# A last stage with two buffers each for mixed values and gates in place of four, and a sixth x1 tile kept in SBUF

## The chip, the core and the metric

The kernel runs on one core of one Trainium2 chip. The metric is the device time of one launch in microseconds, the median of several runs. The engines go by their usual short names: PE (TensorE), DVE (VectorE), ACT (ScalarE), POOL (GpSimd), SP (SyncE). SP computes nothing here: it issues transfers, one after the other, in the order of its program. ACT issues transfers too, between its own instructions. MB below is a million bytes; a tile of 128 partitions by 4,096 float32 values has 2.10 MB, which the profile writes as 2048 KB.

## The reference

The input x is one 512 x 512 image of 64 channels in float32. Two layers are added to it in turn:

```python
x = x + _L0_conv_ref(_gn(x), ...)   # group norm, five projections, einsum, layer norm, output projection, gate
x = x + _L1_conv_ref(_gn(x), ...)   # group norm, 12 x 12 Fourier modes times a complex weight, inverse transform
```

Layer 0 in its core is

```python
left  = (xn @ left_w  + left_b)  * mask * sigmoid(xn @ lgate_w + lgate_b)
right = (xn @ right_w + right_b) * mask * sigmoid(xn @ rgate_w + rgate_b)
out = einsum('bkjd,bkid->bijd', left, right)
out = (_ln(out, onorm_w, onorm_b) @ out_w + out_b) * sigmoid(xn @ ogate_w + ogate_b)
```

Its result x + out is called x1 below. Layer 1 needs sums over the whole of x1 (its low Fourier modes, its squares) before it can add anything to it.

## The kernel before

Five stages run one after the other, each in a block of its own:

- `prepare` reads x for the group norm's statistics and folds weights.
- `project` forms left, right and the output gate, and writes them to HBM (`lr_d`, `gate_d`).
- `contract` does the einsum for one channel after the other (64 of them) and writes the "mixed" values to `mixed_d`.
- `finish_layer0`, the stage that the change is about, forms x1.
- `layer1` takes the spectrum, and then adds the inverse transform to each tile of x1 and stores it to the output.

**SBUF.** The last three stages share one area of 196 KB in each partition, laid out by hand (class `Shared`, line 739; the second argument counts kilobytes). In the last stage but one it holds `XT` = 5 tiles of x (`xt`, 16 KB each, from 0), `MB` = 4 tiles of mixed values (`mt`, 4 KB each, from 80), 4 of gates (`gt`, 4 KB each, from 96), and behind them, from 112, the Fourier rows and smaller things. `contract` uses the bytes from 0 to 96 for its operands, and leaves 96 to 112 free.

**`finish_layer0`.** The image is cut into 128 groups (`GROUPS`) of four image rows, and four groups (`TG`) make one x tile; there are 32 tiles (`TILES`). A group is worked in two halves, and time is counted in slots n, one for each half. Group c needs its mixed values (0.52 MB), its gates (0.52 MB) and a quarter of an x tile (0.52 MB). In slot n:

- DVE does `gate(n)` (L1252), then `scale(n + 2)` (L1244), and in odd slots `add_x` of the group before (L1261). `scale` multiplies mixed values by the norm's scale; `gate` multiplies the projected values by the gates; `add_x` adds the turned result to the x tile, which thereby becomes x1.
- PE does the output projection of half n + 1 (L1154), spreads the norm's scale for half n + 3 (L1149), turns a finished group (L1160) in even slots, and, ten slots behind, does one eighth of the Fourier transform of an x1 tile (L1168).
- ACT squares each finished group (L1199). With the last group of tile k, in slot 8k + 9, it issues the store of that x1 tile to `x1_d` (L1202), if k < `KEPT`: the last `XT` tiles are never stored, and `layer1` takes them from SBUF.
- POOL adds up the squares (L1233).
- SP issues the loads. In odd slots it waits until `scale(n)` is done and loads the mixed values of group n // 2 + `MB` (L771), then waits until `gate(n)` is done and loads the gates of the same group (L774): one load each for the buffer just used. In slots n with n % 8 = 4 it loads x tile n // 8 + 2 (L768), if that is `XT` or above. In slots n with n % 8 = 6, once in seven tiles, it loads Fourier rows (L1137, 672 KB onto 28 partitions).

```python
            def slot(n):
                c = n // 2 + MB
                if n % 2 == 1 and c < GROUPS:
                    sp.wait_ge(m_scaled, n + 1)
                    mid.load_mixed(sp, c)
                    sp.wait_ge(y_gated, n + 1)
                    mid.load_gate(sp, c)
```

On DVE the order is gate(n), scale(n + 2), so in time SP issues the gates of one group and, 0.6 us later, the mixed values of the next. One such pair leaves in each group's time.

**The first loads** are issued in `contract`: the gates of the first `MB` groups and x tiles 0 and 1 beside the last channel (L870 to L875), x tile 2 (L882), the first `MB` mixed tiles (L885), and the x tiles from 3 to `XT` - 1 behind the last small transfers of the scale (L890).

**`layer1`** works through the 32 tiles in the order `TILE`, first those that are still in SBUF. It has `XR` = 10 tile buffers: the `XT` of the stage before and five more. `FREE` = 8: the loads of tiles `XT` to 7 of its order are issued at once (L1376), two more when the columns are ready (L1378), and every later one when a buffer has been stored (L1381).

Of the kernel before, what the change touches and what calls it, by code (L numbers as in the profile page):

```python
# [39 lines left out]
GW = RG * H  # L40
# [1 line left out]
RING = 4  # L42
UB = 2 * BG
UNITS = L // 2
XT = 5
MB = 4
AREA = 196 * 256
DIRECT = 4
BATCH = 7
# [40 lines left out]
class Tools:  # L90


    def __init__(self, nc, ctx, phase):
        self.nc, self.ctx, self.phase = nc, ctx, phase
# [644 lines left out]
class Shared:  # L739

    def __init__(self, t, x, mixed_d, gate_d):
        self.nc = t.nc
        self.base = t.nc.sbuf_base
        t.sb("area", [P, AREA])
        self.xt = [self.at("fi", f"x{b}", 16 * b, [TG, WS, C]) for b in range(XT)]
        self.mt = [self.at("fi", f"m{b}", 80 + 4 * b, [GW]) for b in range(MB)]
        self.gt = [self.at("fi", f"g{b}", 96 + 4 * b, [GW]) for b in range(MB)]
        self.rows = self.at("fi", "rows", 112, [M2, TG * C])
        self.st = self.at("fi", "s", 136, [RG, GW], F32R)
        self.pick = self.at("fi", "pick", 174, [P // 4, P], F32R)  # L750
        self.basis_rows = self.at("fi", "basis_rows", 190, [WS, RG * M2])
        self.x_loaded = [t.sem(f"x_loaded{b}") for b in range(XT)]
        self.m_loaded = [t.sem(f"m_loaded{b}") for b in range(MB)]
        self.g_loaded = [t.sem(f"g_loaded{b}") for b in range(MB)]
        self.s_loaded = t.sem("s_loaded")
        self.basis_loaded = t.sem("basis_loaded")
        self.x_v = x.rearrange("a h w c -> (a h w c)").rearrange("(n g p f) -> n p g f", g=TG, p=P, f=WS * C)
        self.m_v = mixed_d.rearrange("e d (n r) j -> n (e d) (r j)", r=RG)
        self.g_v = gate_d.rearrange("e d (n r) j -> n (e d) (r j)", r=RG)
# [7 lines left out]
    def load_x(self, sp, k):  # L767
        sp.dma_start(self.xt[k % XT].rearrange("p g t c -> p g (t c)"), self.x_v[k]).then_inc(self.x_loaded[k % XT], DMA)  # L768

    def load_mixed(self, sp, c):  # L770
        sp.dma_start(self.mt[c % MB], self.m_v[c]).then_inc(self.m_loaded[c % MB], DMA)  # L771

    def load_gate(self, sp, c):
        sp.dma_start(self.gt[c % MB], self.g_v[c]).then_inc(self.g_loaded[c % MB], DMA)  # L774

# [4 lines left out]
def contract(nc, lr_d, mixed_d, basis_rows, keep, mid):  # L780
# [4 lines left out]
    with ExitStack() as ctx:  # L785
# [63 lines left out]
        def spread_part(eng, part, source, e):  # L849

            for q in range(RG):
                rows = slice(P // 4 * q, P // 4 * q + P // 4)
                at = P // 2 * part + P // 4 * e
                eng.dma_start(mid.st[at:at + P // 4, q, :].bitcast(F32),
                              source[rows, e, :, :].rearrange("p t j -> p (t j)").bitcast(F32)).then_inc(mid.s_loaded, DMA)

        @block.sync
        def _(sp):
# [28 lines left out]
            for e in range(2):  # L887
                sp.wait_ge(low_ready, e + 1)
                spread_part(sp, 1, s_low, e)
            for k in range(3, XT):  # L890
                mid.load_x(sp, k)
# [156 lines left out]
def finish_layer0(nc, x1_d, fourier_d, keep, mid):  # L1048
# [6 lines left out]
    TILES = GROUPS // TG  # L1055
    KEPT = TILES - XT
    with ExitStack() as ctx:
# [16 lines left out]

        x1_stored = [t.sem(f"x1_stored{b}") for b in range(XT)]
        f_stored = [t.sem(f"f_stored{b}") for b in range(2)]
# [206 lines left out]
def layer1(nc, x1_d, w_real, w_imag, inverse_rows, inverse_columns, out, keep, mid):  # L1283
# [7 lines left out]
    GR = L // NG  # L1291
    GP = P // NG
    NTG = GROUPS // TG
    XR = XT + 5
    SPLIT_O = 40
    FREE = XT + 3
    KEPT = NTG - XT
    TILE = [(KEPT + n) % NTG for n in range(NTG)]
    CB = L // GR
    with ExitStack() as ctx:  # L1300
# [17 lines left out]
        col = mid.at("la", "col", 112, [GR, C])  # L1318
        span = TG * WS * C
        xt = [mid.xt[(KEPT + b) % XT].rearrange("p g t c -> p (g t c)") for b in range(XT)]  # L1320
        xt += [mid.at("la", f"x{b}", at, [span]) for b, at in enumerate((80, 96, 176, 144, 160))]
        ps = [t.ps(f"ps{k}", [P, L]) for k in range(8)]
        f_ps = [ps[a][0:C, 0:NM * M2] for a in range(2)]
        s_ps = ps[2][0:C, :]
# [3 lines left out]
        inv_loaded = t.sem("inv_loaded")  # L1328
        loaded = [t.sem(f"loaded{b}") for b in range(XR)]
        stored = [t.sem(f"stored{b}") for b in range(XR)]  # L1330
        step = t.sem("step")
# [21 lines left out]
        def by_group(tile):  # L1353
            return tile.rearrange("p (g f) -> p g f", g=TG)
# [12 lines left out]
        def _(sp):  # L1367
# [5 lines left out]
            def load(n):  # L1373
                sp.dma_start(by_group(xt[n % XR]), x_v[TILE[n]]).then_inc(loaded[n % XR], DMA)

            for n in range(XT, FREE):  # L1376
                load(n)
            sp.wait_ge(col_ready, C // CB)  # L1378
            for n in range(FREE, XR):
                load(n)  # L1380
            for n in range(XR, NTG):  # L1381
                sp.wait_ge(stored[n % XR], DMA * (n // XR))
                load(n)
# [131 lines left out]
def program(nc, ins, tab, out):  # L1515
# [6 lines left out]
    with ExitStack() as ctx:  # L1522
# [28 lines left out]
        with ExitStack() as back:  # L1551
            m = Shared(Tools(nc, back, "back"), x, mixed_d, gate_d)
            contract(nc, lr_d, mixed_d, tab["t_basis_rows"], k, m)
            finish_layer0(nc, x1_d, fourier_d, k, m)
            layer1(nc, x1_d, ins["L1_conv_w_real"], ins["L1_conv_w_imag"], tab["t_inverse_rows"],
                   tab["t_inverse_columns"], out, k, m)
# [20 lines left out]
```

## Time and profile before

| | us |
|---|---|
| median of three runs | 2878.99 |
| lowest and highest run | 2877.46, 2883.83 |
| the profiled execution | 2879.03 |
| its span in the trace | 2877.2 |

| stage | stretch of the span, us |
|---|---|
| `prepare` and `project` | 0 to about 1050 |
| `contract` | to 1828 |
| `finish_layer0` | 1828 to 2498 |
| `layer1` | to 2877 |

The trace is one execution on the core; times in it are counted from the span's start. A transfer has two times: when its queue issues it, and how long after that it has landed; the profile gives the second as "us to landing". "DMA share" in a table of stretches is the mean busy share of the core's 16 DMA engines (it can be a little over 1), and GB/s is what they moved.

### The profile page before, as it was taken

The numbers are of one execution on the slowest core, as the hardware profiler recorded it, in microseconds if no ns is written. First come the engines' busy times: TensorE is split into PE (matmuls) and PEld (weight loads), VectorE is DVE, ScalarE is ACT, GpSimd is POOL, SyncE is SP. The second block draws the span as 40 slices with busy tenths as digits, with TensorE's granted clock in tenths as the row PEclk, the third lists the DMA queues.
The fourth block names the chain that finished last, engine by engine and source line by source line (L and its number), as shares of the span: only waits on it lengthen the run. The fifth ranks groups of instructions, "written<-read, shape, count | busy, mean of one in ns | idle before, by whom it ended". The sixth has DMA issues, their size and how long they took to land. (4 is left out here: it accounts for less than half of the span.)

```text
span 2877.2 us, 44035 instructions
## 1 busy us (share of the span) xinstructions
PE 2459.1 (85%) x14742; PEld 2000.9 (70%) x14742; DVE 2216.7 (77%) x3468; ACT 1380.9 (48%) x1812; POOL 1021.6 (36%) x1043
## 2 busy tenths in 40 slices
PE   0008999889989969999999999599998999979983
PEld 0007998778778858888888887366665666778872
DVE  6998999779779848888888888777676767427852
ACT  0107999779779966676766766122221222100000
POOL 0019988788788820000000000244443444300000
PEclk9999999999999989999999999799999999859996
DMA  9945999888888876777777777999999999539999
GB/s 384 391 166 194 351 349 348 305 329 310 318 310 329 315 274 249 277 280 288 275 287 273 284 281 270 347 391 416 393 415 391 415 384 399 146 126 386 420 421 408
DMA packets 244985, 927.61 MB, mean 322 GB/s; under 512 B 18010, under 2 KB 21594, under 8 KB 244443
## 3 DMA queue, kind: packets, MB, share of 16 engines
q1 hardware_dynamic: 205912, 796.12, 73.4%
q10 hardware_dynamic: 38898, 129.21, 11.3%
q8 instruction: 105, 1.72, 0.2%
q14 instruction: 70, 0.57, 0.1%
HBM read 527.85 MB, written 394.92 MB: 321 GB/s over the span
## 5 line engine op out<-in xcount | busy, mean ns | idle before, releaser
L1233 POOL TENSOR_TENSOR fi_square_sum<-fi_square_sum,fi_square 128x1024 f32<-128x1024 f32 x128 | 302.9, 2366 | 361.1 <-ACT fi_square L1199 361.1
L717 DVE SCALAR_TENSOR_TENSOR pj_lr<-pj_v_ps,keep_b_val,pj_sig 128x1024 f32<-128x1024 f32 x256 | 328.6, 1283 | 128.3 <-PE pj_v_ps L570 97.8
L912 PE MATMUL ct_acc_ps<-ct_l_hi,ct_r_hi 128*128 128x512 f32 x1024 | 404.4, 395 | 26.7 <-DVE ct_r_lo L989 26.7
L914 PE MATMUL ct_acc_ps<-ct_l_hi,ct_r_lo 128*128 128x512 f32 x1024 | 404.2, 395 | 0.0
L913 PE MATMUL ct_acc_ps<-ct_l_lo,ct_r_hi 128*128 128x512 f32 x1024 | 404.2, 395 | 0.0
L1199 ACT ACTIVATE fi_square<-fi_x 128x1024 f32<-128x1024 f32 x128 | 135.5, 1058 | 519.0 <-DVE fi_x L1261 516.5
L510 POOL TENSOR_TENSOR front_ring<-front_ring,front_gn_shift 128x512 f32<-128x512 f32 x256 | 330.4, 1292 | 31.8 <-DVE front_ring L683 31.8
L653 ACT ACTIVATE pj_sig<-pj_g_ps,keep_b_gate 128x1024 f32<-128x1024 f32 x256 | 285.9, 1117 | 42.3 <-PE pj_g_ps L570 37.6
L1154 PE MATMUL fi_y_ps<-fi_scaled,keep_w_bd 128*128 128x512 f32 x512 | 273.5, 616 | 30.0 <-DVE fi_scaled L1244 29.6
L1244 DVE TENSOR_TENSOR fi_scaled<-fi_m,fi_s_ps 128x512 f32<-128x512 f32 x256 | 174.2, 681 | 135.9 <-DMA fi_m<-mixed_d 125.8
L1225 POOL MEMSET fi_square_sum<- 128x1024 f32 x1 | 1.0, 952 | 758.8 <-POOLq L785 758.8
L530 POOL TENSOR_TENSOR front_ring<-front_ring,pj_guess 128x512 f32<-128x512 f32 x256 | 267.7, 1047 | 3.3 <-POOL pj_guess L524 1.6
L1168 PE MATMUL fi_f_ps<-fi_x,fi_basis_rows 128*96 128x256 f32 x1024 | 264.3, 382 | 0.0
L563 PE MATMUL pj_x_ps<-pj_high,front_minus 64*128 64x512 f32 x512 | 257.6, 503 | 0.2
L570 PE MATMUL pj_o_ps<-pj_high,front_w_og_high 64*128 64x512 f32 x512 | 249.4, 487 | 0.1
L912 PEld LDWEIGHTS ct_acc_ps<-ct_l_hi,ct_r_hi 128*128 128x128 f32 x1024 | 198.1, 193 | 68.5 <-issue 27.1
L1430 PE MATMUL la_ps_ps<-la_col,keep_mask_row 128*128 128x256 f32 x1024 | 229.2, 387 | 13.7 <-DVE la_x L1508 9.7
L1149 PE MATMUL fi_s_ps<-fi_s,fi_pick 128*128 128x512 f32 x256 | 208.1, 814 | 36.0 <-DMA fi_s<-ct_s_low 36.0
L692 DVE BATCH_NORM_STATS2 pj_stats<-front_ring 128x6 f32<-128x128 f32 x1024 | 227.6, 287 | 5.4 <-POOL front_ring L510 5.4
L554 PE MATMUL pj_x_ps<-keep_ident,front_ring 64*128 64x64 f32 x2048 | 209.8, 223 | 25.5 <-POOL front_ring L530 24.7
L1430 PEld LDWEIGHTS la_ps_ps<-la_col,keep_mask_row 128*128 128x128 f32 x1024 | 198.2, 194 | 44.5 <-DVE la_x L1508 11.5
L554 PEld LDWEIGHTS pj_x_ps<-keep_ident,front_ring 64*128 64x128 f32 x2048 | 204.3, 140 | 34.2 <-POOL front_ring L530 25.0
(183 smaller groups left out, 6315.1 us busy)
## 6 DMA issues: line engine op xcount, KB each, us to landing
lr_d<-pj_lr SPq DMA_DIRECT2D x128, 1024.0 KB, 6.6
gate_d<-pj_gout SPq DMA_DIRECT2D x128, 512.0 KB, 7.1
ct_l<-lr_d SPq DMA_DIRECT2D x64, 1024.0 KB, 7.0
ct_r<-lr_d SPq DMA_DIRECT2D x64, 1024.0 KB, 9.0
mixed_d<-ct_o SPq DMA_DIRECT2D x64, 1024.0 KB, 5.0
fi_g<-gate_d SPq DMA_DIRECT2D x128, 512.0 KB, 14.8
fi_x<-in_x SPq DMA_DIRECT2D x32, 2048.0 KB, 17.2
fi_m<-mixed_d SPq DMA_DIRECT2D x128, 512.0 KB, 17.5
```

Source lines behind the costliest of these rows:

```text
L510: pool.tensor_tensor(tile(m), tile(m), keep.gn_shift[:, :].unsqueeze(1).to_broadcast([P, WS // 2, C]), ALU.add).then_inc(shifted, 1)
L530: pool.tensor_tensor(tile(m), tile(m), root, ALU.mult).then_inc(xn_ready, 1)
L554: last = pe.matmul(x_ps[m % 2][:, columns], pair, keep.ident[side(e), side(e)], start=(e == 1 and i == 0), stop=False, is_transpose=True, ...
L653: act.activation(sig[m % 2][:, :], g_ps[:, :], ACT.Sigmoid, bias=keep.b_gate[:, 0:1]).then_inc(sig_ready, 1)
L717: dve.scalar_tensor_tensor(out=out[:, :, RG * (m % 2):RG * (m % 2) + RG], in0=v_ps[:, :].rearrange("p (q i) -> p q i", i=RG), scalar=keep. ...
L912: pe.matmul(bank, high, l_hi[b][:, :, k, :], start=(k == 0), stop=False)
L913: pe.matmul(bank, high, l_lo[b][:, :, k, :], start=False, stop=False)
L914: last = pe.matmul(bank, low, l_hi[b][:, :, k, :], start=False, stop=(k == WT - 1))
L1154: pe.matmul(y_ps[n % 2], keep.w2_bd[:, :], scaled[n % 2], start=True, stop=True).then_inc(y_ready, 1)
L1168: last = pe.matmul(f_ps[k % 2], mid.basis_rows[:, s, :], xt[k % XT][:, :, s, :], start=(s == 0), stop=(s == WS - 1))
L1233: pool.tensor_tensor(square_sum[:, :, :], square_sum[:, :, :], square[:, :, :], ALU.add).then_inc(sum_done, 1)
L1430: last = pe.matmul(bank[:, :, s % 2, :], inv_cols[:, s, :], col[:, TG * TILE[n]:TG * TILE[n] + TG, :], start=True, stop=True)
```

## The change

The number of x tiles goes from 5 to 6 and that of the mixed and of the gate tiles from 4 to 2 each. The sixth x tile takes the 16 KB from 80 to 96; the mixed tiles move to 96 and 100, the gate tiles to 104 and 108. `layer1` drops its own tile buffer at 80, and keeps ten in all; `FREE` stays 8. So SP issues a mixed and a gate load two groups ahead in place of four; 26 x1 tiles are stored in place of 27, and 26 are loaded again in `layer1` in place of 27.

```diff
@@ -42,8 +42,8 @@
-XT = 5
-MB = 4
+XT = 6
+MB = 2
 AREA = 196 * 256
@@ -743,8 +743,8 @@
         self.xt = [self.at("fi", f"x{b}", 16 * b, [TG, WS, C]) for b in range(XT)]
-        self.mt = [self.at("fi", f"m{b}", 80 + 4 * b, [GW]) for b in range(MB)]
-        self.gt = [self.at("fi", f"g{b}", 96 + 4 * b, [GW]) for b in range(MB)]
+        self.mt = [self.at("fi", f"m{b}", 96 + 4 * b, [GW]) for b in range(MB)]
+        self.gt = [self.at("fi", f"g{b}", 104 + 4 * b, [GW]) for b in range(MB)]
         self.rows = self.at("fi", "rows", 112, [M2, TG * C])
@@ -1291,9 +1291,9 @@
-    XR = XT + 5
+    XR = XT + 4
     SPLIT_O = 40
-    FREE = XT + 3
+    FREE = XT + 2
@@ -1318,7 +1318,7 @@
         xt = [mid.xt[(KEPT + b) % XT].rearrange("p g t c -> p (g t c)") for b in range(XT)]
-        xt += [mid.at("la", f"x{b}", at, [span]) for b, at in enumerate((80, 96, 176, 144, 160))]
+        xt += [mid.at("la", f"x{b}", at, [span]) for b, at in enumerate((96, 176, 144, 160))]
```

## Rows read from the trace of the kernel before

**Rows 1.** The page: the span, and each engine's busy time.

```profile
span 2877.2 us, 44035 instructions
PE 2459.1 (85%) x14742; PEld 2000.9 (70%) x14742; DVE 2216.7 (77%) x3468; ACT 1380.9 (48%) x1812; POOL 1021.6 (36%) x1043
```

**Rows 2.** Stretches: length, busy time by engine, granted clock, DMA share, GB/s.

```profile
1900.00:1940.00 40.00, 40.00 (x187) 27.98 (x185) 32.31 (x43) 9.23 (x10) 19.50 (x9) 1.00 1.02 414
...
2060.00:2100.00 40.00, 39.28 (x181) 26.77 (x180) 29.24 (x39) 9.20 (x10) 18.25 (x9) 1.00 1.03 417
...
2550.00:2600.00 50.00, 38.11 (x281) 36.69 (x282) 23.92 (x30) 7.12 (x12) 4.37 (x1) 0.70 0.16 57
```

**Rows 3.** Waits, 1830 to 2480: who for whom, us, times, longest.

```profile
DVE fi_scaled L1244 <- DMA fi_m<-mixed_d: 125.8, 59, 8.1
```

**Rows 4.** Timeline of DVE: start, duration; scale at groups 8 and 127.

```profile
1859.76 0.68 DVE L1244 TENSOR_TENSOR fi_scaled<-fi_m,fi_s_ps 128x512 f32<-128x512 f32 x1
...
2477.97 0.68 DVE L1244 TENSOR_TENSOR fi_scaled<-fi_m,fi_s_ps 128x512 f32<-128x512 f32 x1
```

**Rows 5.** Timeline of DVE: scale in three following groups, near 1894.

```profile
1890.37 0.68 DVE L1244 TENSOR_TENSOR fi_scaled<-fi_m,fi_s_ps 128x512 f32<-128x512 f32 x1
...
1893.26 0.68 DVE L1244 TENSOR_TENSOR fi_scaled<-fi_m,fi_s_ps 128x512 f32<-128x512 f32 x1
...
1898.05 0.68 DVE L1244 TENSOR_TENSOR fi_scaled<-fi_m,fi_s_ps 128x512 f32<-128x512 f32 x1
```

**Rows 6.** Timeline of SP's queue, the same place: when transfers are issued.

```profile
1885.69 0.33 SPq L774 DMA_DIRECT2D fi_g<-gate_d  x1
1886.29 0.33 SPq L771 DMA_DIRECT2D fi_m<-mixed_d  x1
...
1890.93 1.14 SPq L768 DMA_DIRECT2D fi_x<-in_x  x1
1892.12 1.43 SPq L771 DMA_DIRECT2D fi_m<-mixed_d  x1
```

**Rows 7.** DMA issues, single: mixed 1886.29, store 1887.43, mixed 1892.12 (KB, us to landing).

```profile
fi_m<-mixed_d SPq DMA_DIRECT2D x1, 512.0 KB, 4.6
...
x_d<-fi_x ACTq DMA_DIRECT2D x1, 2048.0 KB, 9.7
...
fi_m<-mixed_d SPq DMA_DIRECT2D x1, 512.0 KB, 12.0
```

**Rows 8.** Timeline of DVE: scale at the start of groups 114 to 116.

```profile
2417.90 0.69 DVE L1244 TENSOR_TENSOR fi_scaled<-fi_m,fi_s_ps 128x512 f32<-128x512 f32 x1 [3.07 <-DMA fi_m<-mixed_d]
...
2421.55 0.68 DVE L1244 TENSOR_TENSOR fi_scaled<-fi_m,fi_s_ps 128x512 f32<-128x512 f32 x1
...
2425.31 0.68 DVE L1244 TENSOR_TENSOR fi_scaled<-fi_m,fi_s_ps 128x512 f32<-128x512 f32 x1
```

**Rows 9.** Stretches, columns as in Rows 2: a PE gap, and what follows it.

```profile
2177.90:2182.10 4.20, 0.05 (x2) 0.01 (x1) 0.75 (x2) 0.00 (x0) 0.00 (x0) 0.83 1.01 237
...
2182.10:2187.50 5.40, 5.40 (x10) 2.97 (x10) 2.99 (x4) 1.06 (x1) 1.90 (x1) 0.50 0.98 328
2036.90:2040.40 3.50, 0.00 (x1) 0.00 (x0) 0.71 (x2) 0.00 (x0) 0.00 (x0) 1.00 1.02 419
2040.70:2044.10 3.40, 3.40 (x7) 1.80 (x7) 2.72 (x4) 1.06 (x1) 0.17 (x1) 0.50 1.03 418
```

**Rows 10.** Timeline of SP's queue: loads around a load of Fourier rows.

```profile
2013.50 0.79 SPq L774 DMA_DIRECT2D fi_g<-gate_d  x1
2014.39 1.30 SPq L1137 DMA_DIRECT2D fi_rows<-fourier_d  x1
2015.74 0.96 SPq L771 DMA_DIRECT2D fi_m<-mixed_d  x1
```

**Rows 11.** DMA issues, single: the gate load of 2013.50, the mixed load of 2015.74.

```profile
fi_g<-gate_d SPq DMA_DIRECT2D x1, 512.0 KB, 19.5
...
fi_m<-mixed_d SPq DMA_DIRECT2D x1, 512.0 KB, 23.9
```

**Rows 12.** Timeline at the stage's start: x tiles 3 and 4, the next mixed load, scale of group 2.

```profile
1826.36 1.20 SPq L768 DMA_DIRECT2D fi_x<-in_x  x2
...
1831.09 0.34 SPq L771 DMA_DIRECT2D fi_m<-mixed_d  x1
...
1837.21 0.68 DVE L1244 TENSOR_TENSOR fi_scaled<-fi_m,fi_s_ps 128x512 f32<-128x512 f32 x1
```

**Rows 13.** DMA issues, single: the mixed load of 1831.09.

```profile
fi_m<-mixed_d SPq DMA_DIRECT2D x1, 512.0 KB, 9.8
```

## The prediction

> **What bounds the kernel now.** I read the page first [rows 1]. PE is the busiest engine over the whole span, 2459.1 of 2877.2 us, but the change touches one stage and a half, so I went to stretches of that stage [rows 2]. From 1900 to 1940 PE is busy all the time (40.00 of 40.00): PE sets the pace. From 2060 to 2100 it isn't (39.28), DVE neither (29.24), and the DMA engines stand at a share of 1.03 and 417 GB/s: the bytes set the pace. The waits say the same from the other side: DVE's `scale` stood still for mixed values for 125.8 us in 59 waits [rows 3].
>
> The PE's own pace is 4.79 us for a group, read between two starts of `scale`, 1893.26 and 1898.05 [rows 5]. From group 8 to group 127 the stage took 2477.97 - 1859.76 = 618.2 us [rows 4]; 119 groups at 4.79 would be 570.0, so what is lost to DMA today is 48.2 us. The bytes of a tile of four groups are 4.2 MB of mixed values and gates, 2.1 of x and 2.1 of the store: 8.4 MB, 20.1 us at 417 GB/s against 19.2 on PE. Today's stage is thus within a few per cent of both limits, and it gets there because four buffers let requests pile up.
>
> **The change: the wait that it adds.** With two buffers, the mixed load for group c can only leave when `scale` of group c - 2 is done. In the stretch that PE paces, one `scale` ends at 1890.37 + 0.68 = 1891.05, and the `scale` that would need that load starts at 1898.05 [rows 5]: 7.0 us are left for it. With four buffers two more groups, 9.6 us, come on top. How long does such a load take? Alone behind its gate load it lands after 4.6 us, in time. But the mixed load of 1892.12 was issued right behind an x load, with the store of an x1 tile (landing after 9.7) on ACT's queue, and took 12.0 [rows 6, 7]. The queues were nearly empty before it, since the load of 1886.29 needed 4.6. That is the very state in which two buffers would always find them. It landed at 1904.12, that is 6.1 us after 1898.05. Behind the waiting `scale` stand all later DVE instructions of the group; PE waits for their `scaled` and `gated`, and SP's next pair of loads waits for them too. So the waiting shuts off requests: the DMA engines, which have no gap in mid stage today, are idle for a few microseconds in every tile.
>
> **Price of a tile with both an x load and a store.** I take the loop that closes on itself. From the gate load that precedes the store, 1885.69, to the landing at 1904.12 are 18.4 us [rows 6, 7]. The bytes on this way are 0.52 x 4 for two pairs, 2.1 of x and 2.1 of the store: 6.3 MB, 15.1 us at 417 GB/s, so at the very best 15.1 and 2.7 us of fixed time (the load that landed at 1890.89 is 5.2 after 1885.69, with 2.5 us of bytes): 17.8. Then from the late `scale` to the next such gate load: the other half's `scale` and one group more. By DVE's rate after a wait, 3.65 for a group (2417.90 to 2421.55 [rows 8]), that is some 5.0 us; by PE's pace, 4.79, up to 6.8. The loop is 22.8 at best, 24.7 where I take the observed 18.4 and 6.3. I take more than 5.0 because of PE's clock: a PE gap of 4.2 us was followed by 5.4 us at a granted clock of 0.50 and one of 3.5 by 3.4 us at 0.50 [rows 9], which is the lower of its two levels (1.2 in place of 2.4 GHz) and costs half of that stretch, 1.7 to 2.7. The upper end is 18.4 + 6.8 + 1.7, some 27.0. Against 19.2 for four groups of PE, such a tile loses 5.5 us (3.6 to 7.8).
>
> **How many.** x tiles 6 to 31 are now loaded in the stage, at tiles 4 to 29; tiles 0 to 25 are stored, each one tile later. Both fall together at tiles 4 to 26: 23 times 5.5 = 127 us (83 to 179).
>
> **Tiles 27 to 29, an x load and no store.** Gates, x and mixed values are 7.6 us of bytes, and 2.7 fixed, 10.3 after the gate load's issue, where 7.6 are available: 2.7 late. After a wait two groups ran at 3.65 and 3.76 in place of 4.79 [rows 8], which wins back 2.2. I take 1 each, 3 in all (0 to 6). Tiles 1 to 3, with a store alone, I cost at nothing: 1 MB of loads beside the store is covered by the 7.0 us and the 2.2 that can be won back; without that cover it would be some 2 each.
>
> **Fourier rows.** The gate load of 2013.50 landed after 19.5, the mixed load of 2015.74 after 23.9 [rows 10, 11]: 6.6 us apart, with the rows between them, and 1.3 of it the mixed load's own. So the rows hold SP's queue for 5.3 us. Three of the four times this comes one pair behind an x load, where nothing is left to win back: 3 x 5.3 = 16, and 3 for the last one: 19 (12 to 30).
>
> **The start.** x tiles 3 and 4 are issued at 1826.36, the next mixed load at 1831.09 lands 9.8 later, at 1840.9 [rows 12, 13]. Now it is group 2's, which `scale` wants at 1837.21, and x tile 5 (2.1 MB, 5.0 us) is in front of it: 1845.9, so 8.7 us late; 9 (8 to 12). Two gate loads fewer in `contract` move nothing, since PE there waits for the scale.
>
> **What the change saves.** One store of 2.1 MB is 5.0 us of bytes; in a stage whose DMA engines now have gaps that is worth nothing, in today's it would be 5.0. In `layer1` one load is gone, but of those issued before the columns are ready; from 2550 to 2600 the share is 0.16 [rows 2], so it hid in an idle stretch. From there on the stage loads 24 tiles and stores 32, as before. I take 0 (a gain of 5 at most).
>
> **Sum.** 127 + 3 + 19 + 9 = 158 us lost, less the 48.2 lost today: +110, on the profiled execution's 2879.03 (span 2877.2, about 1.8 around it): 2989. That execution is within 0.1 us of the median of the runs, 2878.99. With all low ends: 83 + 0 + 12 + 8 - 48 - 5 = +50, 2929. With all high ends: 179 + 6 + 30 + 12 - 48 = +179, 3058.
>
> **What the notes say.** The Trainium skill ("Trainium Kernel Development and Optimization", Best Practices) advises to double-buffer so that DMA overlaps with compute. By that, two buffers hide the loads and only the saved bytes count; this is the third rival below. The trace speaks against it: 12.0 us of latency stand against 7.0 of lead [rows 5, 7]. The same skill ("Perfetto Trace Analysis", Optimization Strategy) reads a gap that repeats on the engine that should be saturated as a possible lack of buffers; it fits the added wait, not today's, which come at a DMA share of 1.03 [rows 2].
>
> **The rivals.**
> - *The clock holds.* The waits come as I say, but PE's gaps stay short enough, and DVE goes on at its own rate behind each wait: the loop is 18.4 + 5.0 = 23.4, 4.2 a tile, 23 x 4.2 = 97. Sum 97 + 3 + 19 + 9 - 48 = +80, 2959. For it: waits of 3.07 us did not slow the groups behind them [rows 8]. Against it: a PE gap of 3.5 did [rows 9], and my wait is 6.1, of which PE has work left for about two. Chance 0.28.
> - *The clock falls in full each time*, and the loop is 27: 23 x 7.8 = 179, 179 + 3 + 19 + 9 - 48 = +162, 3041. For it: the 4.2 gap cost 2.7. Chance 0.15.
> - *The bytes are the bound anyway, and there are fewer of them.* The requests are fewer at a time but never too few; the stage keeps its pace, and the store that is gone is worth its 5.0: 2874, faster than before. It decides in the loop above: with 5.0 from the late `scale` to the next pair, the way from pair to landing would have to be 20.1 - 5.0 = 15.1, the bare bytes with no fixed time at all. The single trace of it says 18.4. Chance 0.05.
> - *The change doesn't do what it says:* the load that goes was idle time's, the one that comes at the start is not. That part is in my sum (9 us); alone, with no waits, it would give some +4, 2883. Chance 0.03.
>
> **How the numbers follow.** My forecast, 2989, has 0.49. It and the two cases on its sides hold 0.92. The range goes from 2920, below the low ends, to 3060, the high ends; what it leaves out is the last two rivals and a tail above, together some 0.12. This kernel can be told from no change at about 0.2%, 6 us. Faster by more: 0.03, most of the third rival. Within: 0.03. Slower: 0.94.
>
> **What would show it.** In the trace of the changed kernel: waits of DVE's `scale` for mixed loads near 6 us, once in a tile, 250 us or more in total in place of 125.8; a period of `scale` near 24.7 us for four groups in mid stage; a DMA share below 1 and near 350 GB/s there; a median latency of the mixed loads under 10 us in place of 17.5, though each wait is longer; PE's clock at 0.50 for some microseconds in each tile; a first wait of about 9 us in group 2; `layer1` as long as before. I am wrong if the share stays at 1.03 in mid stage, or if the mixed load behind x lands in less than 8 us: then the lead of 7.0 was enough.

## The result

The changed kernel takes 3013.15 us, median of four runs (3007.66 to 3020.91), beside 2878.22 for the kernel before (four runs, 2872.17 to 2883.83): a ratio of 1.0474, 95% interval 1.0457 to 1.0491. That is 135 us slower. The forecast was 110 slower, 2989, in a range of 2920 to 3060. Its profiled execution is the fastest of the four, 3007.66 (span 3005.8), so 128.6 us of span are to be explained.

Nearly all of it lies in `finish_layer0`, whose first `scale` starts 0.8 us earlier than before. From `scale` of group 127 to the end of the span it is 399.2 us in the changed kernel and 399.3 before. From group 8 to group 127 it is 2606.57 - 1871.16 = 735.4 us in place of 618.2 [rows 4]: 117.2 more. The first eight groups take 12.2 more.

The page of the changed kernel, in the lines that answer to [rows 1], with the loads' medians (KB, us to landing):

```profile
span 3005.8 us, 44032 instructions
PE 2500.7 (83%) x14742; PEld 2023.6 (67%) x14742; DVE 2219.6 (74%) x3468; ACT 1379.5 (46%) x1812; POOL 1020.7 (34%) x1043
...
fi_g<-gate_d SPq DMA_DIRECT2D x128, 512.0 KB, 4.7
fi_x<-in_x SPq DMA_DIRECT2D x32, 2048.0 KB, 12.5
fi_m<-mixed_d SPq DMA_DIRECT2D x128, 512.0 KB, 7.0
```

A single mixed load is much quicker than before, 7.0 us in place of 17.5, and the kernel is slower. A latency says nothing until it is held against the lead with which the load was asked for. Stretches of the stage, columns as in [rows 2]:

```profile
2060.00:2100.00 40.00, 29.53 (x110) 19.14 (x111) 21.00 (x29) 5.55 (x6) 11.81 (x5) 0.83 0.87 302
...
2060.00:2400.00 340.00, 280.89 (x1137) 186.72 (x1138) 197.47 (x260) 59.71 (x65) 122.38 (x52) 0.89 0.88 327
```

The longer of them in the kernel before:

```profile
2060.00:2400.00 340.00, 317.90 (x1403) 212.97 (x1402) 237.71 (x318) 72.45 (x79) 150.26 (x64) 0.98 1.02 404
```

No engine is busy all the time now, and neither are the DMA engines: a share of 0.88 and 327 GB/s, where the kernel before has 1.02 and 404 over the same 340 us. The granted clock is 0.89 over the stretch, 0.98 before. The waits of the stage (us in total, times, longest), with [rows 3] for the first; the second and third are PE waiting for DVE's late `scale`:

```profile
DVE fi_scaled L1244 <- DMA fi_m<-mixed_d: 166.8, 36, 9.7
PEld fi_y_ps L1154 <- DVE fi_scaled L1244: 130.3, 36, 9.1
PE fi_y_ps L1154 <- DVE fi_scaled L1244: 115.6, 31, 9.0
DVE fi_gated L1252 <- PE fi_y_ps L1154: 70.8, 81, 2.4
...
DVE fi_gated L1252 <- DMA fi_g<-gate_d: 39.8, 26, 3.3
```

Fewer waits (36 in place of 59), but long ones, and a second kind that the forecast did not have: gates that come late, 26 times.

One turn of the loop, as SP and ACT issue it (start, duration):

```profile
2017.73 0.33 SPq L774 DMA_DIRECT2D fi_g<-gate_d  x1
2018.33 0.33 SPq L771 DMA_DIRECT2D fi_m<-mixed_d  x1
...
2019.47 0.37 ACTq L1202 DMA_DIRECT2D x_d<-fi_x  x1
...
2022.54 0.33 SPq L774 DMA_DIRECT2D fi_g<-gate_d  x1
2022.98 1.11 SPq L768 DMA_DIRECT2D fi_x<-in_x  x1
2024.13 1.44 SPq L771 DMA_DIRECT2D fi_m<-mixed_d  x1
...
2027.93 0.33 SPq L771 DMA_DIRECT2D fi_m<-mixed_d  x1
2038.17 0.33 SPq L774 DMA_DIRECT2D fi_g<-gate_d  x1
...
2044.27 0.33 SPq L774 DMA_DIRECT2D fi_g<-gate_d  x1
```

The same six transfers from 2017.73 to 2024.13, each asked for by itself (KB, us from issue to landing), in that order:

```profile
fi_g<-gate_d SPq DMA_DIRECT2D x1, 512.0 KB, 3.6
fi_m<-mixed_d SPq DMA_DIRECT2D x1, 512.0 KB, 4.8
...
x_d<-fi_x ACTq DMA_DIRECT2D x1, 2048.0 KB, 10.1
fi_g<-gate_d SPq DMA_DIRECT2D x1, 512.0 KB, 8.0
fi_x<-in_x SPq DMA_DIRECT2D x1, 2048.0 KB, 12.5
fi_m<-mixed_d SPq DMA_DIRECT2D x1, 512.0 KB, 12.6
```

And DVE, which waits for the last of them, and before that for the gates (in brackets its idle time and what ended it):

```profile
2030.56 0.75 DVE L1252 SCALAR_TENSOR_TENSOR fi_gated<-fi_y_ps,keep_c_col,fi_g 128x512 f32<-128x512 f32 x1 [1.53 <-DMA fi_g<-gate_d]
2036.79 0.69 DVE L1244 TENSOR_TENSOR fi_scaled<-fi_m,fi_s_ps 128x512 f32<-128x512 f32 x1 [5.48 <-DMA fi_m<-mixed_d]
...
2043.48 0.75 DVE L1252 SCALAR_TENSOR_TENSOR fi_gated<-fi_y_ps,keep_c_col,fi_g 128x512 f32<-128x512 f32 x1 [2.36 <-PE fi_y_ps L1154]
```

From the gate load at 2017.73 to the landing at 2036.7 are 19.0 us, from there to the next such gate load, 2044.27, 7.5: a loop of 26.5. Over 22 such loops in the trace the means are 19.1 and 7.1, 26.2 in all. Between 2027.93 and 2038.17 SP issues nothing: it stands behind DVE.

What PE's clock does meanwhile (stretches; the columns as above):

```profile
2033.30:2037.40 4.10, 0.01 (x1) 0.00 (x0) 0.61 (x2) 0.00 (x0) 0.00 (x0) 0.89 1.03 417
2037.50:2043.30 5.80, 5.77 (x10) 3.04 (x11) 3.62 (x5) 1.06 (x1) 2.27 (x1) 0.50 0.62 218
```

PE stood still for 4.1 us and then worked 5.8 us at a granted clock of 0.50 (1.2 GHz), while the DMA share sank to 0.62 because nothing had been asked for. The trace holds 23 such stretches between groups 8 and 127, 133 us in sum; the kernel before has 4, 20.5 us. In this turn `gate` then waits for PE (the 2.36 above): that is where the clock gets onto the path.

### The profile page after: what moved, and what is told of

The parts are those of the page before. It is cut to its first block and busy times, and to the rows that moved or that the text cites. A ratio compares the mean times of both kernels' runs of the same rounds, so it can differ in the third digit from the quotient of the medians.

```text
span 3005.8 us, 44032 instructions
## 1 busy us (share of the span) xinstructions
PE 2500.7 (83%) x14742; PEld 2023.6 (67%) x14742; DVE 2219.6 (74%) x3468; ACT 1379.5 (46%) x1812; POOL 1020.7 (34%) x1043
## 3 DMA queue, kind: packets, MB, share of 16 engines
q1 hardware_dynamic: 205384, 794.02, 70.8%
## 5 line engine op out<-in xcount | busy, mean ns | idle before, releaser
L1154 PE MATMUL fi_y_ps<-fi_scaled,keep_w_bd 128*128 128x512 f32 x512 | 300.3, 672 | 115.7 <-DVE fi_scaled L1244 115.6
L1244 DVE TENSOR_TENSOR fi_scaled<-fi_m,fi_s_ps 128x512 f32<-128x512 f32 x256 | 173.9, 680 | 175.7 <-DMA fi_m<-mixed_d 166.8
L1252 DVE SCALAR_TENSOR_TENSOR fi_gated<-fi_y_ps,keep_c_col,fi_g 128x512 f32<-128x512 f32 x256 | 191.7, 749 | 134.0 <-PE fi_y_ps L1154 70.8
L1168 PE MATMUL fi_f_ps<-fi_x,fi_basis_rows 128*96 128x256 f32 x1024 | 279.2, 399 | 0.0
L1149 PE MATMUL fi_s_ps<-fi_s,fi_pick 128*128 128x512 f32 x256 | 224.2, 876 | 36.0 <-DMA fi_s<-ct_s_low 36.0
L554 PE MATMUL pj_x_ps<-keep_ident,front_ring 64*128 64x64 f32 x2048 | 209.7, 223 | 25.4 <-POOL front_ring L530 24.7
```

What stands on the lines that cost most here:

```text
L1154: pe.matmul(y_ps[n % 2], keep.w2_bd[:, :], scaled[n % 2], start=True, stop=True).then_inc(y_ready, 1)
L1168: last = pe.matmul(f_ps[k % 2], mid.basis_rows[:, s, :], xt[k % XT][:, :, s, :], start=(s == 0), stop=(s == WS - 1))
```

## The experiments

All times are medians. Gains and losses are told as distances to the kernel before on the same chip: the changed kernel is 135 us above it. The ratio is to the kernel before on the same chip. Its median was 2873.3 beside the first four experiments (both kernels with five tiles, x loads in quarters in front, x loads on ACT's queue), 2874.0 beside the next four (small x loads, small stores, sixth tile later, all spread), and 2875.5 beside the last four. "Period" is the time from one `scale` to the one four groups later, as a mean over the 21 tiles from group 20 to group 103, those with Fourier rows included: 21.3 us in the kernel before, 26.2 in the changed one. The small x loads and the small stores leave something out of the result; all other kernels compute all of it. "Start" is the time from the first `scale` to that of group 8: 30.0 before, 42.2 changed.

| kernel | us | ratio (95%) | period | start |
|---|---|---|---|---|
| the change | 3013.2 | 1.0474 (1.0457 to 1.0491) | 26.2 | 42.2 |
| two buffers, five tiles | 3019.2 | 1.0497 (1.0473 to 1.0520) | 26.6 | 38.3 |
| three buffers, five tiles | 2886.7 | 1.0046 (1.0029 to 1.0063) | 21.8 | 29.6 |
| x loads in quarters, in front | 2962.2 | 1.0308 (1.0290 to 1.0325) | 24.7 | 42.6 |
| x loads on ACT's queue | 2917.6 | 1.0156 (1.0139 to 1.0173) | 22.3 | 42.8 |
| small x loads | 2856.7 | 0.9941 (0.9926 to 0.9956) | 19.9 | 42.7 |
| small stores | 2884.6 | 1.0038 (1.0024 to 1.0051) | 21.0 | 39.0 |
| sixth tile later | 3003.8 | 1.0475 (1.0454 to 1.0495) | 26.2 | 40.7 |
| all spread | 2887.7 | 1.0051 (1.0037 to 1.0064) | 21.5 | 38.5 |
| stores in quarters | 3016.3 | 1.0487 (1.0470 to 1.0504) | 26.6 | 43.8 |
| x loads in quarters, behind | 2908.7 | 1.0112 (1.0096 to 1.0127) | 22.3 | 41.6 |
| all spread, ahead | 2881.1 | 1.0022 (1.0012 to 1.0031) | 21.1 | 37.8 |
| the same, four buffers, five tiles | 2874.3 | 0.9997 (0.9988 to 1.0007) | 21.1 | 28.8 |

### Which part of the change

Two buffers alone, and three:

```diff
-MB = 4
+MB = 2        # XT stays 5
```

> The kernel before with two buffers each for mixed values and gates, and still five x tiles: the change without its sixth tile. Theory (a lead of about 7 us for a mixed load that takes 12 to 14 behind an x load, beside a store): the whole loss is there, less the late start of the changed kernel (11 us), plus two more tiles with both an x load and a store at some 6.5 us each: 3010 to 3020. Rival A (the sixth tile's load, ahead of the first mixed loads, and its new places are what costs): it falls back to 2880 to 2900.

Measured 3019.2, as expected: the loss is all there without the sixth tile. Rival A falls; neither the sixth tile nor the new places of the buffers are what costs, and the tiles run at 26.6 us.

```diff
-MB = 4
+MB = 3        # XT stays 5
```

> The kernel before with three buffers each, and five x tiles. Theory: the lead grows by one group, to about 11.8 us, against 12 to 14; what is left, 1 to 2 us a tile, is won back by two quick groups, so the bytes bind again: 2878 to 2892. Rival B (the time goes with the number of bytes that can be under way, whatever their order): about half of the loss of two buffers stays, near 2945.

Measured 2886.7, inside the 2878 to 2892 of the theory, far from rival B's 2945. In the stretch from 2060 to 2400 the DMA share is back:

```profile
2060.00:2400.00 340.00, 310.38 (x1389) 211.38 (x1387) 237.48 (x314) 70.91 (x78) 149.31 (x64) 0.99 1.02 394
```

One buffer of each kind carries nearly all of the difference between 2 and 4: the distance to the kernel before is 146 us with two, 13 with three, 0 with four. The lead doesn't have to pass the latency for that. With more requests under way the mixed load behind x takes 14.4 us here (median of 22), against a lead of some 11.8, and DVE waits for it some 4 us in most tiles (33 waits, 113.4 us in all). Most of that is won back by the quick groups behind it.

### Is it the x load in front?

```diff
-                if n % TH == 4 and XT <= k < TILES:      # whole, 2.1 MB
-                    ...
-                    mid.load_x(sp, k)
+                k, part = (n - 4) // TH + 2, (n - 4) % TH // 2
+                if n % 2 == 0 and XT <= k < TILES:       # a quarter, in each group
+                    ...
+                    mid.load_quarter(sp, k, part)
```

> The changed kernel with each later x load cut into four of 0.52 MB, one in each group, so that never more than 0.52 MB of x is in front of a mixed load; same buffers, same bytes. Theory: a mixed load lands 6 us after its issue, with the store beside it 8 to 10, of which the part above 7 is mostly won back; the period of a tile falls from 26 to 20.5 to 22, and with the late start of 11 the kernel takes 2885 to 2920. Rival B (only the bytes that can be under way count): no more than a fifth comes back, 2985 or above.

Measured 2962.2, 89 us above the kernel before: between the two, and a miss for both. A third of the loss came back, not three quarters. DVE's waits for mixed values became many (80) and short, and their sum didn't fall (200.8 us): the quarter is still in front of each mixed load, and the store now takes 15.3 us (mean). Mixed loads that run beside it for over 2 us take 9.8 (median), more than the lead, the others 6.0.

```profile
DVE fi_scaled L1249 <- DMA fi_m<-mixed_d: 200.8, 80, 9.8
```

The same quarters behind the mixed load of their group:

```diff
                     mid.load_mixed(sp, c)
+                k, part = (n - 5) // TH + 2, (n - 5) % TH // 2
+                if n % 2 == 1 and XT <= k < TILES:
+                    ...
+                    mid.load_quarter(sp, k, part)
+                if n % 2 == 1 and c < GROUPS:
                     sp.wait_ge(y_gated, n + 1)
                     mid.load_gate(sp, c)
-                ...                                      # the whole x load
```

> The changed kernel with the later x loads in quarters, each behind the mixed load of its group in place of in front; stores whole. Theory: against the quarters in front (2962) each mixed load has 1.3 us less in front of it, 2.6 while the store runs: a period of 22 to 23.5 in place of 24.7, 2925 to 2950. If the order within a group is of no weight: 2962.

Measured 2908.7, 33 us above the kernel before, period 22.3, better still than expected: 56 us for the order of two transfers. The waits for mixed values are down to 93.6; those for gates are up to 65.1, from 12.2 with the quarters in front:

```profile
DVE fi_scaled L1250 <- DMA fi_m<-mixed_d: 93.6, 71, 9.7
...
DVE fi_gated L1258 <- DMA fi_g<-gate_d: 65.1, 39, 2.9
```

Another way to get x out of the mixed load's way is another queue:

```diff
         def _(act):
             def slot(n):
+                k = n // TH + 2
+                if n % TH == 4 and XT <= k < TILES:
+                    ...                                  # the same three waits
+                    mid.load_x(act, k)
```

> The changed kernel with the later x loads issued by ACT in place of SP, at the same slots, whole. They are then behind the store on ACT's queue, and beside the mixed loads, not in front of them. Theory: a gate and a mixed load get half of the DMA engines, 5.0 + 2.7 = 7.7 us from the gate load's issue against 7.6 available; the waits nearly go, the period is 20.3 to 21.5: 2885 to 2910. Rival B: as for the quartered loads, 2985 or above.

Measured 2917.6, 44 us above the kernel before and 8 above the expected range, with the period at 22.3 in place of 20.3 to 21.5: the theory's direction and most of its size; not all waits went (124.5 us for mixed values, 59.6 for gates). With a whole x load still in the system, only its place in the queues was changed, and 91 us came back. So the number of bytes that may be under way isn't what causes most of the loss.

### The two large transfers by themselves

```diff
-                    mid.load_x(sp, k)
+                    sp.dma_start(mid.xt[k % XT][:, 0, 0, :], mid.x_v[k][:, 0, 0:C])...
```

> The changed kernel with every x load that the last but one stage issues itself (tiles 6 to 31) shrunk from 2.1 MB to 0.03 MB; same place, same waits. It leaves that part of x out of the result. Theory (the x load in front of the mixed load is what makes it late): with the store alone the tiles go at 18.7 to 19.3 us as tiles 1 to 3 of the changed kernel do, and only the start (11 us) and the Fourier rows cost: 2860 to 2875. If the store by itself holds a gate or mixed load over its 7 us so long that it isn't won back, the period stays over 21: above 2910.

Measured 2856.7, 3 us under the range. The period is 19.9, with tiles without Fourier rows at 18.4 to 20.4, and the granted clock never falls between groups 8 and 127. Without the x load there is no loss. By itself this doesn't tell the load's place from its bytes, since 26 loads of 2.1 MB are gone as well; the runs that keep all bytes and move or cut the x load do.

```diff
-                        act.dma_start(x1_v[k], xt[k % XT]...)
+                        act.dma_start(x1_v[k][:, 0, 0:C], xt[k % XT][:, 0, 0, :])...
```

> The changed kernel with every x1 store shrunk from 2.1 MB to 0.03 MB, and the last stage loading the same number of bytes from x in place of x1. It leaves layer 0 out of those 26 tiles of the result. Theory: without the store a mixed load behind x lands 10.3 us after its gate load's issue, 2.7 late, and 2.2 are won back: a period of 19.7 to 20.7 like the changed kernel's last tiles, 2870 to 2900. Rival C (the x load alone does it, the store is beside the point): the period stays above 24, 2950 or more.

Measured 2884.6, as expected (2870 to 2900), and rival C falls: behind the x load alone a mixed load is late by little more than two quick groups win back (waits of 2.2 to 3.3 us in most tiles). It takes both: over the 570.0 us of PE's pace for groups 8 to 127, this kernel loses 47 (616.7), the one with small x loads 15 (585.2), and the changed kernel 165.

Then the store in quarters, the x load whole:

```diff
-                    if g % TG == TG - 1 and k < KEPT:
-                        act.dma_start(x1_v[k], xt[k % XT]...)
+                    if k < KEPT:
+                        act.dma_start(x1_v[k][:, g % TG, :], xt[k % XT][:, g % TG, :, :]...)
```

> The changed kernel with the x1 stores cut into quarters, one behind each group; x loads whole and in front of the mixed load as before. Theory: of the 19 us from gate load to landing, the part of the store that runs beside it falls from 5.0 to 1.3 to 2.6 us; the wait falls by as much and the period to 22 to 24: 2930 to 2970. If the store's size is beside the point: 3013.

Measured 3016.3: nothing is gained. My expectation was wrong, and its own trace tells why. The x load and the mixed load behind it take as long as before or longer:

```profile
fi_x<-in_x SPq DMA_DIRECT2D x1, 2048.0 KB, 13.8
...
fi_m<-mixed_d SPq DMA_DIRECT2D x1, 512.0 KB, 14.5
```

Over its loops the way from the first gate load to the landing is 19.5 us, the rest 7.1. A loop's store comes to the same 2.1 MB whether cut or not, and in 19.5 us at least three of its quarters are issued; they pass beside the x load as the whole did. The gates gain (their waits are down from 39.8 to 9.1 us), the mixed values lose as much (up from 166.8 to 208.8). Cutting a transfer helped here only where other loads got in front of its parts.

### The start

```diff
-            for k in range(3, XT):
+            for k in range(3, XT - 1):
                 mid.load_x(sp, k)
...
+                if n % 2 == 0 and n < 2 * TG:
+                    mid.load_quarter(sp, XT - 1, n // 2)
```

> The changed kernel with the first load of the sixth x tile taken from in front of the first mixed load of the stage, and issued in four parts in the first four groups. Theory: the wait of about 9 us in group 2 goes, some of it comes back as 1 to 2 us in the first groups, and the rest is as it was: 8 to 11 us less than the changed kernel, 3002 to 3006. If the start didn't count (won back later): no change, 3013.

Measured 3003.8, but on its own chip the ratio is 1.0475 (1.0454 to 1.0495), that of the changed kernel: in time it can't be told from it. In the trace the start is 40.7 us in place of 42.2, so 1.5 of the expected 8 to 11 came back. What I had missed: x tiles 3 and 4 are in front of group 2's mixed load too. They landed it at 1840.9 before [rows 12, 13], where it was group 4's; as group 2's, wanted at 1837.21, that is already 3.7 late, and the first quarter adds its own 1.3. So 3.9 us came back in group 2, and 2.4 of them went again up to group 8: group 5's mixed load, for one, now behind a quarter, takes 7.0 us in place of 4.3.

### Everything spread

Quarters behind the mixed loads, stores in quarters, and the sixth tile later, in one kernel:

> Two buffers each and six x tiles, with all transfers spread: x loads in quarters, one in each group and behind its mixed load, x1 stored in quarters as each group is done, and the sixth tile loaded late as above. Nothing is left out. Theory: gate and mixed load are 5.2 us, with a share of 0.5 MB of store 6.5 against 7.0 to 7.6: no waits for the lead; the bytes bind at 20.1 us a tile, one store less: 2865 to 2890. Rival B (two buffers can't keep the DMA engines busy however the bytes are spread): above 2940, as the quartered loads with whole stores gave 2962.

Measured 2887.7 (1.0051), inside the expected 2865 to 2890, with nothing left out and two buffers. The stage runs at the bytes' pace again, as the stretch of 2060 to 2400 shows:

```profile
2060.00:2400.00 340.00, 325.60 (x1417) 213.81 (x1417) 245.59 (x324) 72.79 (x81) 152.26 (x65) 0.98 1.02 404
```

Rival B ("two buffers can't keep the DMA engines busy however the bytes are spread") falls: the distance to the kernel before is 14 us in place of 135. In its mid stage a gate load takes 7.0 us and a mixed load 8.2 (medians, 2100 to 2125), just about the lead. The expectation of no waits failed: DVE waits for mixed values 99 times, 122.6 us in all, but 4.6 at most.

```profile
x_d<-fi_x ACTq DMA_DIRECT2D x5, 512.0 KB, 6.8
fi_g<-gate_d SPq DMA_DIRECT2D x5, 512.0 KB, 7.0
fi_m<-mixed_d SPq DMA_DIRECT2D x5, 512.0 KB, 8.2
fi_x<-in_x SPq DMA_DIRECT2D x5, 512.0 KB, 9.1
```

Two steps further: x quarters from the fourth tile on are issued three tiles ahead, and the Fourier rows on ACT's queue.

```diff
-            for k in range(3, XT):                       # in contract
-                mid.load_x(sp, k)
...
+                k, part = (n - 3) // TH + 3, (n - 3) % TH // 2
+                if n % 2 == 1 and 3 <= k < TILES:
+                    ...
+                    mid.load_quarter(sp, k, part)
...
+                    act.dma_start(mid.rows[rows, :, :], rows_v[rows, :, :]).then_inc(rows_loaded, DMA)
```

> Two buffers each, six x tiles, all transfers spread as in the run before, and two things more: every x tile from the fourth on is loaded in quarters during the tile three before its use, none at the stage's start, and ACT issues the loads of the Fourier rows. Nothing is left out. Theory: the start loses nothing (8 us less than the spread kernel), idle DMA time of the first tiles is used (up to 5), and the rows no longer stand in front of mixed loads (3 times 3 to 6): 2855 to 2872, faster than both kernels. If two buffers still cost something, it stays above 2874.

Measured 2881.1 (1.0022, 1.0012 to 1.0031), 6 us above the kernel before where the spread kernel is 14, so the expected 2855 to 2872 was missed. (Its profiled execution took 2890.15, 9 above the median; 7 to 8 of them lie in `contract`, ahead of all that this version changes.) The start is 37.8 in place of 30.0; there DVE goes at 3.65 us a group, the lead of two buffers is shorter by the same 1.1 to 1.7 a group, and the spread transfers take 6 to 10. The tiles with rows still take 24.0 to 24.6.

And the change taken out of that kernel:

> The spread kernel of the first run of this call, with four buffers each and five x tiles in place of two and six: the change taken out of it, all else the same. Theory: once the transfers are spread, the lead is no longer short, and what the sixth tile saves (one store of 2.1 MB, 5.0 us, where the bytes bind) is all that is left: 0 to 5 us slower than that run, 2857 to 2877. If two buffers still cost, this one is the faster.

Measured 2874.3 (0.9997): 6.8 us faster than with two buffers and six tiles, where 0 to 5 slower was expected, and equal to the kernel before. Two buffers still cost something. The difference is in the start (28.8 and 37.8); the period is 21.1 in both. The 5 us of the store that is saved can't be seen, since group 8 to group 127 takes 617.6 us with six tiles and 615.5 with five. And spreading the transfers brings nothing where the lead is long. No version that computes the whole result beats the kernel before.

## Why the prediction was right

The mechanism was right: the mixed load behind x, beside a store, lands after its lead, once in a tile, and the wait shuts off the requests. The measured loss, 128.6 us in the profiled execution, is 17% over the sum of 110 (135 between the medians, 23%). That it is so near is in part luck, since two errors of opposite sign met: the turn with x load and store costs 6.8 us a tile in place of 5.5 (29 too little over 23 tiles), the Fourier rows cost 5.5 us in place of 19 (some 13 too much). Term by term:

- **The lead and the latency.** Forecast: 7.0 us of lead, 12.0 of latency, late by about 6. The trace has 12.6 of latency and a wait of 5.48 in the turn shown.
- **The loop with x load and store.** Forecast 18.4 + 6.3 = 24.7, measured 19.1 + 7.1 = 26.2. This is the term that was too small. The first part came from one observed case and the mean is 0.7 longer. The second I put between 5.0 and 6.8 + 1.7; it follows the clock. Behind the 23 late landings it is 6.0 to 6.3 in the 7 turns where the clock was low for 3.4 us, 6.9 to 7.5 in the 13 where it was 6.8, and 8.0 to 9.0 in the 3 with Fourier rows. In the two turns behind them, where the clock held, it is 5.0: the 5.0 that the forecast took from DVE's rate. The run with small stores has both kinds behind waits of like length (`scale` and the next such gate load, then the stretch from the wait's end; first a turn in which the clock held, then one in which it fell):

```profile
2347.98 0.69 DVE L1244 TENSOR_TENSOR fi_scaled<-fi_m,fi_s_ps 128x512 f32<-128x512 f32 x1 [5.65 <-DMA fi_m<-mixed_d]
2353.00 0.33 SPq L774 DMA_DIRECT2D fi_g<-gate_d  x1
2348.70:2353.00 4.30, 4.28 (x20) 2.96 (x21) 4.30 (x7) 1.06 (x1) 0.77 (x1) 1.00 0.63 217
...
2430.37 0.69 DVE L1244 TENSOR_TENSOR fi_scaled<-fi_m,fi_s_ps 128x512 f32<-128x512 f32 x1 [5.02 <-DMA fi_m<-mixed_d]
2436.69 0.33 SPq L774 DMA_DIRECT2D fi_g<-gate_d  x1
2431.10:2436.70 5.60, 5.59 (x17) 3.42 (x18) 4.38 (x7) 1.06 (x1) 2.09 (x1) 0.70 0.57 198
```

That is 5.0 and 6.3 us, so 3.4 us at 0.50 cost 1.3, and 6.8 us cost 1.9 to 2.5. I had counted with 1.3 in the forecast's 6.3, and the clock was low for the longer time in most turns. No run changed the clock alone; these turns, side by side, are what there is.
- **The 23 tiles.** Forecast 127 for them and 16 for three loads of Fourier rows, 143. Measured 601.9 us for 23 tiles, less 23 x 19.16: 161. In it the rows cost less than I said: the tile behind a load of rows takes 27.8, the others 25.9, so 1.8 each in place of 5.3. With the x loads in quarters behind the mixed ones the same difference is 4.7 (26.3 and 21.6), in the kernel before 7.3 (27.6 and 20.3): behind a late x load the rows' own delay is in part hidden.
- **Tiles 27 to 29.** Forecast 3, measured 22.7 + 20.7 + 19.7 less 57.5: 5.6. The last load of rows: forecast 3, measured nothing.
- **The start.** Forecast 9, measured 12.2; the wait in group 2 itself is 9.7 (the longest above). The rest is a late gate load beside the first store, 3.3, in tile 1, which I had costed at nothing.
- **`layer1`.** Forecast 0, measured -0.1.
- **What is lost today.** 48.2, as read.

161 + 5.6 + 12.2 - 48.2 is 130.6. Small remainders, of tiles 2 and 3 and the last groups (-1.4) and of the stage's beginning (-0.8), bring it to the 128.6.

Of the marks that I set: mixed latency under 10 (7.0), a share well below 1 (0.88 and 327 GB/s, I had said 350), clock at 0.50 in each tile (23 times), a first wait near 9 (9.7), `layer1` unchanged. One mark failed: waits of `scale` of 250 us or more. They are 166.8: 23 waits behind an x load beside a store with 133, the one in group 2 with 9.7, and 24 in twelve others. The forecast gives no working for its 250. It is about today's 125.8 with the 127 of the tiles on top; but today's waits are gone, not still there beneath the new ones, and a part of the loss is now DVE waiting for gates (39.8) and for PE (70.8).

The first rival (the clock holds, 2959) and the second (it falls in full, 3041) lie on the two sides of the result, and the result is between the forecast and the second. The third, fewer bytes and nothing else, said 2874, and falls: 3013. So does the fourth (no waits, the start alone, 2883). It had the advice of the Trainium skill on its side ("Trainium Kernel Development and Optimization", Best Practices: double-buffer, so that DMA and compute overlap). Here two buffers fell 135 us short of four with 2.1 MB transfers in the same queue and beside it, and 14 with the same bytes spread evenly (2887.7), most of it in the start.

## What to carry to other kernels

Count the buffers of a stream not by what it uses but by the largest thing that can stand in front of its load: the lead in microseconds (from the instruction that frees a buffer to the one that needs the next) has to reach the latency with the big transfer ahead and the store beside, but for what the engines can win back. With two buffers DVE waited some 5.6 us a tile, and they cost 135 to 146 us; with three some 4, and they cost 13. Where memory is short, order and cut the transfers before giving up a buffer: quarters behind the small load were worth some 100 us here, in front 46, a cut store nothing. And the saved store (5.0 us of bytes) could be seen in no run, neither in the changed kernel, whose DMA engines have gaps, nor with all transfers spread.

## What the runs showed of the hardware

- A small load beside a whole store of 2.1 MB lands about when the store does. The gate load of 2022.54 (0.52 MB, the mixed load in front of it landed 0.6 us later) took 8.0 us, where the one of 2017.73 took 3.6; the store, issued 3.1 us before it, landed at 2029.6, the gate load at 2030.5. In 22 such turns it took 7.1 to 9.5 us, and landed from 1.6 us before the store to 2.1 after it. At half of the 417 GB/s it would take some 4.9 (an estimate: the 3.6 and once more the 1.3 us of its bytes). With the store in quarters the same load takes 5.5 (median, 4.4 to 6.9), with small stores 3.9. How the DMA engines come to this isn't shown.
- That is the source of the 26 late gates, and not the x load right behind the gate load: with small x loads the gates' waits are still there (first line), with small stores they are gone (second line; us in total, times, longest).

```profile
DVE fi_gated L1252 <- DMA fi_g<-gate_d: 48.0, 27, 3.8
...
DVE fi_gated L1252 <- DMA fi_g<-gate_d: 0.8, 2, 0.4
```

- The granted clock fell to 0.50 in each of the 23 tiles in which PE stood still for 3.5 to 6.0 us, and stayed there for 3.4 or 6.8 us. In the run with small x loads, where PE's longest gap in the stage is 3.0 us, it did not fall once. The gap's length alone doesn't decide: in the kernel before it fell behind one of 2.1 us and held behind one of 2.2, and with small stores it held behind one of 3.3.
